# Fewer semaphore counts by TensorE, and steps of VectorE, TensorE and ScalarE put in another order, in a two-layer graph network

## The chip, the cores and the metric

One core of a Trainium2 chip runs the whole program. The metric is the device time of one execution in microseconds (us). Three runs of the kernel before gave 1814.47, 1814.22 and 1812.03 us; their median is 1814.22 us.

## The reference

A graph of 3125 nodes with 64 features and 100000 edges, sorted by their destination, goes through two layers. Cut to what matters:

```python
# layer 0 (16 edge features, edge type 0..2, node type 0..1)
h1, h2, h3, h4 = (projection of x by the node's type, for W1..W4)
w5e   = edge_feat @ W5[edge_type] + b5[edge_type]
num   = sum(h3[dst] * (h4[src] + w5e), axis=-1)
score = softmax((num / 4)[:, None], axis=-1)[:, 0]
out   = h1 + segment_sum(score[:, None] * (h2[src] + w5e), dst)
x     = layernorm(x + out)
# layer 1 (32 edge features)
m     = relu(x[src] + edge_feats @ We + be) + 1e-7
a     = exp(m - segment_max(m, dst)[dst]) / its segment_sum
x     = layernorm(x + (x + segment_sum(m * a, dst)) @ Wm + bm)
```

All arithmetic on the features is float32; rows that are fetched by a product with a one-hot matrix are split in three bf16 parts.

## The kernel before

The edges are cut in two halves, and a chunk is 512 edges of each half: channels of the first half lie on partitions 0 to 63, those of the second on 64 to 127. There are `CHUNKS` = 98 chunks (49 for each of two sets of buffers, s = c % 2, r = c // 2). Sums over the edges of a node are running scans along the edges, whose last value is fetched per node at the end.

Each engine has its own program, written out by hand, and waits on semaphores: an instruction adds to one as it ends, and another engine waits for a count. Names of semaphores say what has ended, such as `q4_ready`, `num_ready`, `runT`.

**Stage 0** (layer 0) is a loop over c on each engine, one chunk a step, with work of several chunks in each step.

- GpSimd fetches the source rows of chunk c with indirect DMAs (`gather0`, L599), 8 of them, or 6 where a quarter of the rows comes by a one-hot product (56 chunks, `PICKED`). A ring of 8 buffers lies between it and TensorE.
- TensorE in step c: `pick0` (L872, one-hot products, about 19 matmuls of 512 columns a step), `project0` of chunk c+1 (L881 and, by `add_rows`, L854 and L859), `turn_inj` of c+1 (L894), `numerator` of c (L909, turns the product for VectorE), `difference` of c (L854, L859 again), `turn_prob` of c-1 (L918), `turn_run` of c-2 (L927).
- VectorE in step c: `score_parts` of c-1 (L1184, L1187, L1190), `mask` of c+1 (L1196), `expand` of c (L1205, a scan), `products` of c (L1213), `probabilities` of c-1 (L1218, L1220, L1223), `message_sums` of c-2 (L1229, L1235, a scan), and then `one_hot0` (L1178, six or seven tiles) that a later `pick0` reads.
- ScalarE in step c: `exponents` of c-1 (L677), `copy_keep` of c (L690), which waits for the scan of c-2, `widen` of c-1 (L683), `copy_q2` of c (L696), `copy_picked` (L707), and `store0` of c-2 (L713), which copies what `turn_run` made and issues its DMA.

**Stage 1** (layer 1) is such a loop again, from c = -2 to 98.

- TensorE: `pick` (L970), `project1` of c+2 (L949, L952, L958), `turn1` of c-1 (L981), which turns two scans of 512 columns, first the sum of weights, then the sum of weighted messages.
- VectorE: `of_part` (L1294, every second step: takes the right half of a pair of one-hot rows), `maxima` of c (L1328, L1333, L1337), `summands` of c-1 (L1343), `one_hot` (L1285), `sums` of c-1 (two scans, L1353, L1358).
- ScalarE: `decays`, `store_max` and `decay` of c (L766 to L782), `store1` of c-1 (L789, two copies and a DMA), `messages` of c+2 (L759, L761, the relu that `maxima` of c+2 reads two steps later).

The lines that set the order are these two of stage 0 (TensorE, VectorE), and the last three calls of ScalarE's step in stage 1:

```python
for work, d in ((project0, 1), (turn_inj, 1), (numerator, 0), (difference, 0), (turn_prob, -1), (turn_run, -2)):
for work, d in ((score_parts, -1), (mask, 1), (expand, 0), (products, 0), (probabilities, -1), (message_sums, -2)):
```

## Time and profile before

| | |
|---|---|
| median of three runs | 1814.22 us (1812.03 to 1814.47) |
| profiled execution, span from its first to its last instruction | 2243.3 us |
| mean granted TensorE clock in it | 0.901 |
| TensorE matmuls, busy | 1756.8 us (78%), 8720 instructions |
| VectorE, busy | 1622.9 us (72%), 3313 instructions |
| GpSimd, busy | 1321.5 us (59%), 1377 instructions |
| ScalarE, busy | 785.0 us (35%), 1508 instructions |

The own time of the profiled execution is its span, 2243.3 us; what lies around the span is not told, and can only add to it. It is 429 us above the median of the runs that are not profiled. So a wait in the profile need not be in the runs at the same length, and how much of each can be in them is a question of its own. Busy times of matmuls are modelled and overlap; the starts of two matmuls tell what one costs. "remote" marks a wait that ended with a semaphore count for which no instruction that had just ended is found; "issue" marks an idle time that no wait in the profile explains.

### The profile page before, as it was taken

To read this page: it belongs to the slowest core of one execution; us is meant where nothing else is said; L and a number is where in the kernel's file an instruction comes from. 1 tells how busy PE (TensorE), PEld (TensorE's weight loads), DVE (VectorE), ACT (ScalarE), POOL (GpSimd) and SP (SyncE) were. 2 spreads that over 40 slices of the span, in tenths; PEclk is the share of its full clock that TensorE was granted. 3 is DMA by queue.
4 is the path that set the end of the run, shared out by engine and by line. 5 is a ranking of instruction groups with operands and counts; after the bars stand their busy time and mean duration, and the time that the engine had idled before them with its cause. 6 is when DMAs were issued, how large, how long until landed. Compare 5 with 4: busy or idle time off the path is not lost.

```text
span 2243.3 us, 28657 instructions
## 1 busy us (share of the span) xinstructions
PE 1756.8 (78%) x8720; PEld 1065.5 (47%) x8720; DVE 1622.9 (72%) x3313; ACT 785.0 (35%) x1508; POOL 1321.5 (59%) x1377
## 2 busy tenths in 40 slices
PE   4447988888788887889875278888888889888864
PEld 4423555555555554555544135444444545445434
DVE  6042777778777777777768558788878878879785
ACT  3110222222222222223222135555545545455551
POOL 5661566666666666666650666666666666666624
PEclk9988998999999999999987579899998999999875
DMA  7951454445454544545443235555545555555441
GB/s 252 342 129 48 124 144 131 146 138 151 135 142 146 141 148 138 148 140 147 139 128 111 53 86 154 149 152 157 157 144 158 161 141 169 150 162 155 142 145 44
DMA packets 216628, 322.18 MB, mean 144 GB/s; under 512 B 62017, under 2 KB 124026, under 8 KB 216347
## 3 DMA queue, kind: packets, MB, share of 16 engines
q1 hardware_dynamic: 128556, 147.55, 22.1%
q0 software_dynamic: 44016, 70.01, 13.6%
q10 hardware_dynamic: 43904, 102.79, 13.0%
q8 instruction: 71, 1.16, 0.2%
q14 instruction: 81, 0.66, 0.1%
HBM read 186.93 MB, written 133.22 MB: 143 GB/s over the span
## 4 chain that ended last, share of the span: by engine, by line
PE 32%; DVE 25%; issue 17%; another core or an unknown queue 15%; ACT 8%; ACTq 1%; POOL 1%; DMA 1%; DVEq 0%; SPq 0%; POOLq 0%
PE wide L970 13%; PE wide L872 5%; DVE h3d L1205 4%; PE wide L981 4%; DVE run L1235 4%; DVE late L1178 4%; DVE edge_lists L1178 3%; DVE score L1184 2%; PE bank L949 2%; DVE prod L1213 2%; ACT block L789 2%; DVE bank L1229 2%; PE bank L958 2%; PE bank L833 1%
## 5 line engine op out<-in xcount | busy, mean ns | idle before, releaser
L609 POOL DMA_INDIRECT rows<-d_x,idx x588 | 558.8, 950 | 323.0 <-issue 154.1
L599 POOL DMA_INDIRECT block<-d_h,idx x496 | 476.4, 960 | 265.0 <-issue 131.4
L970 PE MATMUL wide<-late,ntype_i 125*128 125x512 bf16 x975 | 235.2, 399 | 51.1 <-DVE ntype_i L1318 49.7
L872 PE MATMUL wide<-late,typed 125*128 125x512 bf16 x728 | 234.2, 403 | 39.0 <-issue 19.7
L599 POOL DMA_INDIRECT rows<-d_h,idx x176 | 169.0, 960 | 155.2 <-PE wide L859 51.7
L970 PE MATMUL wide<-edge_lists,ntype_i 125*128 125x512 bf16 x936 | 233.4, 406 | 9.6 <-issue 9.4
L872 PE MATMUL wide<-edge_lists,typed 125*128 125x512 bf16 x672 | 210.8, 395 | 2.8 <-issue 2.7
L981 PE MATMUL wide<-ident,block 128*128 128x128 f32 x784 | 147.3, 317 | 73.1 <-issue 56.5
L789 ACT ACTIVATE block<-wide 128x512 f32<-128x512 f32 x196 | 108.3, 592 | 266.8 <-remote 214.1
L1184 DVE TENSOR_REDUCE score<-bank 128x8 f32<-128x512 f32 x98 | 67.4, 688 | 177.9 <-remote 165.7
L690 ACT ACTIVATE keep_late<-keep 128x512 bf16<-128x512 bf16 x98 | 61.7, 630 | 353.1 <-DVE run L1235 240.8
L970 PEld LDWEIGHTS wide<-late,ntype_i 125*128 125x128 bf16 x975 | 100.1, 103 | 168.6 <-DVE ntype_i L1318 50.1
L696 ACT ACTIVATE q_sb<-wide 128x512 f32<-128x512 f32 x98 | 58.4, 596 | 299.8 <-remote 270.6
L981 PEld LDWEIGHTS wide<-ident,block 128*128 128x128 f32 x784 | 115.9, 210 | 99.6 <-issue 80.4
L970 PEld LDWEIGHTS wide<-edge_lists,ntype_i 125*128 125x128 bf16 x936 | 97.5, 104 | 130.0 <-issue 42.0
L918 PE MATMUL bank<-ident,prob_wide 128*128 128x128 f32 x392 | 67.5, 298 | 113.8 <-issue 84.6
L872 PE MATMUL wide<-late,ntype_i 125*128 125x512 bf16 x364 | 145.4, 400 | 5.4 <-issue 5.2
L872 PEld LDWEIGHTS wide<-late,typed 125*128 125x128 bf16 x728 | 74.4, 103 | 128.4 <-issue 63.0
L872 PE MATMUL wide<-edge_lists,ntype_i 125*128 125x512 bf16 x336 | 132.1, 393 | 2.0 <-issue 2.0
L1205 DVE TENSOR_TENSOR_SCAN h3d<-keep,h3d,bank 128x512 f32<-128x512 bf16 x98 | 124.8, 1274 | 8.7 <-PE bank L894 8.7
L1178 DVE TENSOR_SCALAR late<-msg,pick_of 125x512 bf16<-125x512 f16 x364 | 113.8, 376 | 21.0 <-PE wide L872 10.8
L1333 DVE TENSOR_TENSOR_SCAN h3d<-bank,h3d,keep 128x511 f32<-128x511 f32 x98 | 125.5, 1281 | 3.5
(227 smaller groups left out, 3503.6 us busy)
## 6 DMA issues: line engine op xcount, KB each, us to landing
d_run<-block ACTq DMA_DIRECT2D x98, 512.0 KB
d_inj<-zeros SPq DMA_DIRECT2D x28, 896.0 KB
inj<-d_inj SPq DMA_DIRECT2D x98, 256.0 KB
d_run<-stage ACTq DMA_DIRECT2D x98, 256.0 KB
feat<-in_ea16x3T SPq DMA_DIRECT2D x196, 96.0 KB
types<-d_type SPq DMA_DIRECT2D x196, 64.0 KB
keep<-d_keep SPq DMA_DIRECT2D x196, 64.0 KB
keep<-d_pen SPq DMA_DIRECT2D x196, 64.0 KB
```

The source lines that it names most:

```text
L599: pool.indirect_dma_start(out=ring[c % RING][:, j, h, :], out_offset=None, in_=d_h24, in_offset=bass.IndirectOffsetOnAxis(ap=idx[:, c, at: ...
L609: pool.indirect_dma_start(out=rows1[c % RING1][:, j, h, :], out_offset=None, in_=d_x1, in_offset=bass.IndirectOffsetOnAxis(ap=idx[:, c, at ...
L789: act.activation(stage1[s][:, :, :, q, :], p_out1[:, q * CH:(q + 1) * CH].rearrange("p (j h c) -> p j h c", j=TILES, h=2), ACT.Copy).then_ ...
L872: ins = pe.matmul(p_pick[s][:, 0:cols], table0[n][:, k, :], hot0[b][:, k - b * KT, 0:cols], start=(k == 0 and n == 0), stop=(k == NT - 1 a ...
L918: ins = pe.matmul(p_prob[:, j:CH:TILES], prob_wide[s][:, j, :, :].rearrange("p h c -> p (h c)"), ident[:, :], is_transpose=True, start=Tru ...
L970: ins = pe.matmul(p_hot[s], table[q][:, SPLIT * k:SPLIT * (k + 1), :].rearrange("p b c -> p (b c)"), hot[s][:, k, :], start=(k == 0 and q ...
L981: ins = pe.matmul(p_out1[:, q * CH + j * P:q * CH + (j + 1) * P], src[:, j:CH:TILES], ident[:, :], is_transpose=True, start=True, stop=True)
L1178: ins = dve.tensor_scalar(hot0[b][:, k - b * KT, 0:cols], pick_slots[u % SLOTS][0:NP, 0:cols], pick_of[:, k:k + 1], None, ALU.is_equal)
L1184: dve.tensor_reduce(score[s][:, :, :, :].rearrange("p j h a -> p (j h a)"), p_num[:, :].rearrange("p (e c) -> p e c", c=C), AX.X, ALU.add) ...
L1205: dve.tensor_tensor_scan(h3d[s][:, :], keep[s][:, :], p_inj[:, :], h3d[1 - s][:, CH - 1:CH], ALU.mult, ALU.add).then_inc(h3_ready[s], 1)
L1235: dve.tensor_tensor_scan(run[s][:, :], keep_late[s][:, :], p_prob[:, :], run[1 - s][:, CH - 1:CH], ALU.mult, ALU.add).then_inc(run_ready[s ...
L1333: dve.tensor_tensor_scan(before[s][:, 1:CH], p_m[c % 3][:, 0:CH - 1], keep[s][:, 1:CH], before[s][:, 0:1], ALU.max, ALU.add).then_inc(befo ...
```

## The change

In stage 0 TensorE no longer counts `q4_ready` (but for the last chunk, `last_rows`), `num_ready`, and `runT` (but for the last chunk, `last_turned`). Who waited for them waits for a count that TensorE makes a little later anyway: `mask` for `injT`, `score_parts` and `products` for `q2_ready`, `store0` for `probT` of the next chunk. In stage 1 `turn1` counts once for both halves (`turned`) in place of twice, and ScalarE's `store1` waits for both before its first copy. The orders change too: VectorE's stage 0 step begins with `expand` and `products`, and `message_sums` stands ahead of `probabilities`; TensorE's has `turn_run` ahead of `turn_prob`; in stage 1 VectorE does `maxima` ahead of `of_part` (the half selection), and ScalarE does `messages` (the relu) ahead of `store1`. The diff, cut to its core:

```diff
             def store0(s, r, c):
-                act.wait_ge(runT[s], r + 1)
+                if c == CHUNKS - 1:
+                    act.wait_ge(last_turned, 1)
+                else:
+                    act.wait_ge(probT[1 - s], r + s + 1)
...
             def store1(s, r, c):
                 act.wait_ge(stored[s], 16 * (EACH + r))
+                act.wait_ge(turned[s], r + 1)
                 for q in range(2):
-                    act.wait_ge(runT[s], EACH + 2 * r + q + 1)
...
+                if c + 2 < CHUNKS:
+                    messages(*chunk_of(c + 2))
                 if c >= 1:
                     store1(*chunk_of(c - 1))
-                if c + 2 < CHUNKS:
-                    messages(*chunk_of(c + 2))
...
-                add_rows(s, c, 1).then_inc(q4_ready[s], 1)
+                ins = add_rows(s, c, 1)
+                if c == CHUNKS - 1:
+                    ins.then_inc(last_rows, 1)
...
             def difference(s, r, c):
 
-                pe.wait_ge(prod_ready[s], r + 1)
                 add_rows(s, c, 0).then_inc(q2_ready[s], 1)
...
-                ins.then_inc(num_ready[s], 1)
...
-                ins.then_inc(runT[s], 1)
+                if c == CHUNKS - 1:
+                    ins.then_inc(last_turned, 1)
...
-                for work, d in ((project0, 1), (turn_inj, 1), (numerator, 0), (difference, 0), (turn_prob, -1), (turn_run, -2)):
+                for work, d in ((project0, 1), (turn_inj, 1), (numerator, 0), (difference, 0), (turn_run, -2), (turn_prob, -1)):
...
-                    ins.then_inc(runT[s], 1)
+                ins.then_inc(turned[s], 1)
...
             def score_parts(s, r, c):
 
-                dve.wait_ge(num_ready[s], r + 1)
+                dve.wait_ge(q2_ready[s], r + 1)
...
-                wait(dve, q4_ready[s], r)
+                wait(dve, injT[s], r)
...
                 dve.wait_ge(h3_ready[s], r + 1)
-                dve.wait_ge(q4_ready[s], r + 1)
-                wait(dve, num_ready[s], r)
+                if c == CHUNKS - 1:
+                    dve.wait_ge(last_rows, 1)
+                wait(dve, q2_ready[s], r)
...
-                wait(dve, runT[s], r)
...
-                for work, d in ((score_parts, -1), (mask, 1), (expand, 0), (products, 0), (probabilities, -1), (message_sums, -2)):
+                for work, d in ((expand, 0), (products, 0), (mask, 1), (score_parts, -1), (message_sums, -2), (probabilities, -1)):
...
             for c in range(-2, CHUNKS + 1):
+                if 0 <= c < CHUNKS:
+                    maxima(*chunk_of(c))
                 if c % 2 == 0 and (c + 2) // 2 < PAIRS:
                     of_part((c + 2) // 2)
-                if 0 <= c < CHUNKS:
-                    maxima(*chunk_of(c))
```

On VectorE a step in the middle of stage 0 reads so before, from one group of one-hot tiles (`edge_lists`) back to `score`:

```order
L1184 TENSOR_REDUCE score<-bank 128x8
L1187 TENSOR_REDUCE top<-score 128x8
L1190 TENSOR_TENSOR diff<-score,top 128x8
L1196 SCALAR_TENSOR_TENSOR featm<-types,type_of_row,feat 128x512
L1205 SCALAR_TENSOR_TENSOR h3d<-keep,h3d,bank 128x512
L1213 SCALAR_TENSOR_TENSOR prod<-h3d,wide 128x512
L1218 TENSOR_REDUCE total<-expo 128x8
L1220 RECIPROCAL inv<-total 128x8
L1223 TENSOR_TENSOR prob<-expo,inv 128x8
L1229 TENSOR_TENSOR bank<-bank,q_sb 128x512
L1235 SCALAR_TENSOR_TENSOR run<-keep_late,run,bank 128x512
L1178 TENSOR_SCALAR edge_lists<-msg,pick_of 125x512 x7
```

and so in the changed kernel (its line numbers are a little higher):

```order
L1210 SCALAR_TENSOR_TENSOR h3d<-keep,h3d,bank 128x512
L1219 SCALAR_TENSOR_TENSOR prod<-h3d,wide 128x512
L1201 SCALAR_TENSOR_TENSOR featm<-types,type_of_row,feat 128x512
L1189 TENSOR_REDUCE score<-bank 128x8
L1192 TENSOR_REDUCE top<-score 128x8
L1195 TENSOR_TENSOR diff<-score,top 128x8
L1235 TENSOR_TENSOR bank<-bank,q_sb 128x512
L1240 SCALAR_TENSOR_TENSOR run<-keep_late,run,bank 128x512
L1224 TENSOR_REDUCE total<-expo 128x8
L1226 RECIPROCAL inv<-total 128x8
L1229 TENSOR_TENSOR prob<-expo,inv 128x8
L1183 TENSOR_SCALAR edge_lists<-msg,pick_of 125x512 x7
```

The score, which reads what TensorE's `numerator` turned, moved from the first place to the fourth, and the three small instructions of the probabilities moved behind the scan of the messages, next to the one-hot tiles.

On ScalarE in the middle of stage 1 (`block` is the staged output and one of the relu buffers, `bank` the messages in PSUM), before:

```order
L782 DMA d_own<-block 64x512
L776 ACTIVATE bank<-prob_wide 128x512
L789 ACTIVATE block<-wide 128x8x64 x2
L792 DMA d_run<-block 128x1024
L759 ACTIVATE block<-bank 64x512
L761 ACTIVATE bank<-bank 128x512
L766 ACTIVATE prob_wide<-q_sb 128x512
```

and in the changed kernel:

```order
L786 DMA d_own<-block 64x512
L780 ACTIVATE bank<-prob_wide 128x512
L763 ACTIVATE block<-bank 64x512
L765 ACTIVATE bank<-bank 128x512
L793 ACTIVATE block<-wide 128x8x64 x2
L796 DMA d_run<-block 128x1024
L770 ACTIVATE prob_wide<-q_sb 128x512
```

The two relu instructions stand ahead of the two copies and their DMA now. The same instructions are issued on every engine as before.

## Rows read from the trace of the kernel before

**Rows 1.** The page: the span, and busy time, share and instructions of two engines.
```profile
span 2243.3 us, 28657 instructions
PE 1756.8 (78%) x8720; PEld 1065.5 (47%) x8720; DVE 1622.9 (72%) x3313; ACT 785.0 (35%) x1508; POOL 1321.5 (59%) x1377
```
**Rows 2.** Stretches of the two loops: us, each engine's busy us (instructions), clock, DMA.
```profile
226.00:1213.00 987.00, 838.91 (x4477) 526.37 (x4476) 750.73 (x1671) 272.63 (x581) 592.43 (x616) 0.94 0.49 141
1305.00:2175.00 870.00, 738.87 (x3479) 418.91 (x3478) 706.29 (x1231) 452.31 (x779) 533.72 (x564) 0.91 0.52 151
```
**Rows 3.** Who waited for whom: engine, line, releaser: us in total, times, longest.
```profile
DVE h3d L1328 <- ACT bank L761: 101.0, 19, 9.3
ACT block L789 <- remote: 214.1, 55, 8.1
POOL block L599 <- issue: 131.4, 431, 0.3
```
**Rows 4.** The chain that ended last, in stage 0: start, us, what.
```profile
709.16 3.92 another core or an unknown queue
...
721.30 0.86 another core or an unknown queue
722.19 0.69 DVE score L1184
...
730.38 3.86 another core or an unknown queue
```
**Rows 5.** Timeline in stage 0: start, us, engine, line, operation, count, [idle before].
```profile
706.44 1.02 PE L881 MATMUL wide<-featm,w 128*128 128x512 f32 x2
...
708.20 0.64 PE L909 MATMUL bank<-ident,prod 128*128 128x128 f32 x4
...
709.26 0.60 PE L918 MATMUL bank<-ident,prob_wide 128*128 128x128 f32 x4
709.70 0.64 PE L927 MATMUL bank<-ident,run 128*128 128x128 f32 x4
710.18 0.60 PE L872 MATMUL wide<-late,typed 125*128 125x512 bf16 x2
...
710.62 0.38 PE L872 MATMUL wide<-late,ntype_i 125*128 125x512 bf16 x1
...
713.10 0.69 DVE L1184 TENSOR_REDUCE score<-bank 128x8 f32<-128x512 f32 x1 [3.94 <-remote]
```
**Rows 6.** Timeline: the end of the next step, on VectorE, ScalarE and TensorE.
```profile
719.12 2.18 DVE L1178 TENSOR_SCALAR edge_lists<-msg,pick_of 125x512 bf16<-125x512 f16 x7
719.30 0.63 ACT L690 ACTIVATE keep_late<-keep 128x512 bf16<-128x512 bf16 x1 [2.87 <-DVE run L1235]
...
719.84 0.61 ACT L683 ACTIVATE prob_wide<-prob 128x512 f32<-128x512 f32 x1
...
720.50 0.95 PE L918 MATMUL bank<-ident,prob_wide 128*128 128x128 f32 x4 [2.45 <-issue]
```
**Rows 7.** Groups of VectorE's instructions in the stretch 226 to 1213 us.
```profile
L1205 DVE TENSOR_TENSOR_SCAN h3d<-keep,h3d,bank 128x512 f32<-128x512 bf16 x98 | 124.8, 1274 | 8.7 <-PE bank L894 8.7
...
L1196 DVE SCALAR_TENSOR_TENSOR featm<-types,type_of_row,feat 128x512 f32<-128x512 bf16 x96 | 71.7, 747 | 0.5 <-issue 0.3
L1184 DVE TENSOR_REDUCE score<-bank 128x8 f32<-128x512 f32 x97 | 66.7, 688 | 177.9 <-remote 165.7 <-PE bank L909 12.2
L1213 DVE SCALAR_TENSOR_TENSOR prod<-h3d,wide 128x512 f32<-128x512 f32 x97 | 66.6, 687 | 3.3
...
L1220 DVE RECIPROCAL inv<-total 128x8 f32<-128x8 f32 x96 | 19.5, 203 | 3.3
...
L1223 DVE TENSOR_TENSOR prob<-expo,inv 128x8 f32<-128x8 f32 x96 | 16.0, 167 | 3.3
...
L1218 DVE TENSOR_REDUCE total<-expo 128x8 f32<-128x8 f32 x96 | 14.8, 154 | 33.4 <-issue 19.0 <-ACT expo L677 14.2
```
**Rows 8.** Timeline of VectorE in stage 1: the first instruction of two steps.
```profile
1510.52 0.21 DVE L1328 SCALAR_TENSOR_TENSOR h3d<-bank,h3d,keep 128x1 f32<-128x1 f32 x1
...
1517.73 0.19 DVE L1328 SCALAR_TENSOR_TENSOR h3d<-bank,h3d,keep 128x1 f32<-128x1 f32 x1
```

More of the change, by code:

```diff
@@ L289, in gnn_program @@
         feat_in, keep_in, inj_in = sems("feat_in"), sems("keep_in"), sems("inj_in")
-        masked, q4_ready, q2_ready, injT = sems("masked"), sems("q4_ready"), sems("q2_ready"), sems("injT")
+        masked, q2_ready, injT, last_rows = sems("masked"), sems("q2_ready"), sems("injT"), sem("last_rows")
         keep_copied, q2_copied, h3_ready, prod_ready = sems("keep_copied"), sems("q2_copied"), sems("h3_ready"), sems("prod_ready")
-        num_ready, score_ready, diff_ready = sems("num_ready"), sems("score_ready"), sems("diff_ready")
+        score_ready, diff_ready = sems("score_ready"), sems("diff_ready")
         exps_ready, prob_ready = sems("exps_ready"), sems("prob_ready")
@@ L295, in gnn_program @@
         wide_ready, probT, msg_ready = sems("wide_ready"), sems("probT"), sems("msg_ready")
-        run_ready, runT, staged, stored = sems("run_ready"), sems("runT"), sems("staged"), sems("stored")
+        run_ready, staged, stored = sems("run_ready"), sems("staged"), sems("stored")
+        last_turned, turned = sem("last_turned"), sems("turned")
         s_cut, s_square, s_squared, s_var, s_sqrt, s_x1, s_x1_out = (sem("s_cut"), sem("s_square"), sem("s_squared"),
@@ L908, in numerator @@
                 for j in range(TILES):
-                    ins = pe.matmul(p_num[:, j * P:(j + 1) * P], prod[s][:, j:CH:TILES], ident[:, :], is_transpose=True,
-                                    start=True, stop=True)
-                ins.then_inc(num_ready[s], 1)
+                    pe.matmul(p_num[:, j * P:(j + 1) * P], prod[s][:, j:CH:TILES], ident[:, :], is_transpose=True,
+                              start=True, stop=True)
             def turn_prob(s, r, c):
@@ L936, in _ @@
                     pick0(AHEAD_PIECES + c + 1)
-                for work, d in ((project0, 1), (turn_inj, 1), (numerator, 0), (difference, 0), (turn_prob, -1), (turn_run, -2)):
+                for work, d in ((project0, 1), (turn_inj, 1), (numerator, 0), (difference, 0), (turn_run, -2), (turn_prob, -1)):
                     if chunk_of(c + d):
                         work(*chunk_of(c + d))
-            for work, back in ((numerator, 2), (difference, 2), (turn_prob, 3), (turn_run, 4), (turn_inj, 1), (project0, 1),
-                               (turn_prob, 2), (numerator, 1), (difference, 1), (turn_run, 3), (turn_run, 2), (turn_prob, 1), (turn_run, 1)):
+            for work, back in ((numerator, 2), (difference, 2), (turn_run, 4), (turn_prob, 3), (turn_inj, 1), (project0, 1),
+                               (turn_run, 3), (turn_prob, 2), (numerator, 1), (difference, 1), (turn_run, 2), (turn_prob, 1), (turn_run, 1)):
                 work(*chunk_of(CHUNKS - back))
@@ L1349, in sums @@
                 dve.wait_ge(decay_ready[s], r + 1)
-                dve.wait_ge(runT[s], EACH + 2 * r)
+                wait(dve, turned[s], r)
                 if not first:
```

## The prediction

> **What bounds the kernel now.** I first compare the profiled execution with the runs. Its span is 2243.3 us [rows 1], 429 more than the median of 1814.22, so I ask of every wait whether the runs can hold it. A measurement of this kernel tells about 0.2% (3.6 us) from no change.
>
> The stretches come next [rows 2]. The loop of stage 0 takes 987 us for 98 steps, 10.07 a step, and VectorE is busy for 750.7 of it; that of stage 1 takes 870, 8.88 a step, with VectorE busy for 706.3. So VectorE idles 236 us in the one and 164 in the other, 400 in all. Outside the loops lie 386 us, with 166 of VectorE's work.
>
> What a step costs without a wait: on VectorE the chain goes from the score at 722.19 to the end of seven one-hot tiles at 730.38, 8.19 us; the mean is 6.2 tiles (611 tiles, of about 0.31 us each by 2.18 for seven in rows 6), so 7.95. On TensorE all but the one-hot products goes from 706.44 to 710.18, 3.74 us with no gap [rows 5]; about 19 one-hot products a step at 0.22 a start (710.18 to 710.62 for two) add 4.18: 7.92. GpSimd has 616 gathers in the stretch, 592.4 us busy, with 131.4 / 431 = 0.305 us of issue for each [rows 2, 3]: 780 us, 7.96 a step. Three engines need 7.9 to 8.0 us each. In stage 1 VectorE goes from 1510.52 to 1517.73 with no wait, 7.21 us [rows 8].
>
> With no wait in either loop the span would be 2243.3 - (987 - 98 × 7.95) - (870 - 98 × 7.21) = 2243.3 - 208 - 163 = 1872 us. **The runs are below even that, by 58 us.** So most of the waits that the profile shows are not in the runs, and the balance of three engines leaves little to win.
>
> What the waits are: VectorE's score waits 177.9 us, 165.7 of it for a "remote" count [rows 7]. The chain has it alternate, 3.9 us, 0.9 us, 3.9 us [rows 4]. The place shows that it is a late count: the numerator's four matmuls start at 708.20 and take 0.64 in all, yet the score starts at 713.10 [rows 5], 4.3 us after their end, while TensorE already runs the next one-hot products. Here the count travels slowly in the profiled execution. ScalarE waits 214.1 us in the same way in front of `store1`, and `messages` stands behind it, for which VectorE waits 101.0 us [rows 3].
>
> **The change part by part.**
>
> *Counts taken away.* TensorE drops 97 counts of `q4_ready`, 98 of `num_ready`, 97 of `runT` and 98 of stage 1's second, 390 in all. A block of four transposes has a count on its last. The block at 709.26 lasts 0.60, three starts and one matmul of 0.27, so its starts lie 0.11 apart; the next block starts 0.44 after it, again 0.11 for each of four. For the block at 709.70 it is 0.64, 0.12 apart, and 0.48 to the next work [rows 5]. The start behind a counted matmul is no later than the others, within 0.01 us. I cost a count at 0; the bounds are 0 and 390 × 0.01 = 4 us. The Trainium skill (TensorE: Matmul & The Clock Gate, The cost: per-tile semaphore tail) has increments of concurrent tiles go one after another at about 26.3 ns each; an estimate by it is 390 × 26.3 ns = 10.3 us less. The rows do not show that spacing.
>
> *Score to the fourth place.* The numerator's count is now wanted behind `expand`, `products` and `mask`: 1.27 + 0.69 + 0.75 = 2.7 us later [rows 7]; waiting for `q2_ready` in its place makes it about 0.48 later (TensorE's block of `difference`, as long as that at 709.70), so 2.2 us of cover are won for this count. But a step waits for its latest count, and what is late next is known: `expand`, now first, wants `injT` of its chunk. TensorE makes that count in the same step as the old one, one block (0.44 us) sooner, and VectorE asks for it 0.52 us later after its scan, since the probabilities stand in between (next part). So a late count costs 0.96 us less than before: of waits of 3.9 us 2.9 are left, those of 0.9 vanish [rows 4]. With as many of the one as of the other that is about 0.9 us a step, 88 us of the 178 [rows 7]. Bounds: 0.44 a step, 43 us, if the later asking is no gain; all 178, if the counts are less late once fewer are made.
>
> *Probabilities behind the message sums.* `widen` on ScalarE stands behind `copy_keep`, which waits for the scan: copy at 719.30, widen at 719.84 [rows 6]. The probabilities now end 0.154 + 0.203 + 0.167 = 0.52 us after the scan [rows 7], about when ScalarE is free of the copy (0.54). Cost 0, at most 0.1 a step, 10 us. The one-hot tiles end 0.52 later against the scan.
>
> *`turn_run` ahead of `turn_prob`.* It fills TensorE's wait for `widen` (2.45 us at 720.50 [rows 6]) with 0.48 us of work. TensorE is then at the next `pick0` 0.48 sooner, and finds the one-hot tiles 0.52 later. The two cancel: 0 in the likeliest case. `store0` waits for `probT` in place of `runT`, which now ends the same group: 0.
>
> *Stage 1.* `messages` ahead of `store1` frees VectorE's 101.0 us [rows 3] from a count that only `store1` needs. `store1` starts its first copy one half later, about 0.5 us, with nobody but a DMA behind it: 0. `maxima` ahead of `of_part` lets 2 us of work pass over a late `picked` count; the product that needs `of_part` stands behind four us of one-hot products on TensorE: 0. `decays` behind `store1` are as they were.
>
> **The sum.** In the profiled execution's own time the change is worth 88 us of stage 0's wait (43 to 178) and 101 of stage 1's, less what comes back (I allow a third of the 101), so I expect its span near 2060 to 2090 us. The runs hold a part of that only. Above: the stretches outside the loops hold at least VectorE's 166 us, so the loops take 1648 us or less in a run, against 1487 with no wait: 161 us of waits at most. Below: 0, since the runs are 58 us under the span with no wait. I take 25 us, near the low end, because the row that is nearest, the 58, already asks for shorter work outside the loops than the profile has. Of 400 us of idle time the change relieves 88 + 101 = 189, 47%: 12 us. **1814 - 12 = 1802 us.**
>
> **The rivals.**
>
> *The runs have no such waits at all.* Then every engine does the same work, and 1814 comes out again, within 3 us. For it: the 58 us. Against it: two balanced engines that wait for each other in both directions seldom lose nothing. Chance 0.22.
>
> *The late counts are in the runs too.* If idle time shrank alike everywhere, the runs would keep (1814 - 1623) / (2243 - 1623) = 31% of it: 123 us in the loops, 47% of it relieved, 58 us: 1756. Against it: outside the loops the idle time is mostly of DMAs and gathers, which have no reason to shrink to a third. Chance 0.07.
>
> *The counts cost TensorE time themselves.* If it paced the loops and each count took what the nearest rows could hide (0.01 us) the gain were 4 us, 1810; by the estimate from the Trainium skill's page above, 1804. Rows 5 speak against it. Chance 0.03.
>
> *Slower: `pick0` waits for its one-hot tiles.* They end 0.52 us later after the scan. If TensorE paces a step and doesn't use the 0.48 us that it gains, because it never waited for `widen` in the runs, each step can lose 0.04 to 0.52 us: 4 to 51 over 98 steps. It decides as soon as TensorE finishes a step ahead of the tiles with no wait at `turn_prob`. I take 0.12, of short steps mixed with long: 12 us, 1826. For it: the three engines are within 0.1 us a step, and whatever ties TensorE closer to VectorE's end costs. Chance 0.16.
>
> The forecast has the other 0.52, and its own range is 1780 to 1810.
>
> **How the numbers follow.** Faster: 0.50 of the forecast's 0.52, with 0.07 and 0.03: 0.60. Same: 0.02 of it and 0.20 of the 0.22: 0.22. Slower: 0.16 and 0.02: 0.18. The range leaves out the large gain and the worst third of the slower case: from 1776 (a gain of 38, the forecast with 80 us of waits in the runs) to 1826.
>
> **What would show it.** In the changed profile the score should wait under 30 us, and the first place, `expand`, for `injT` some 90 (43 to 135 would fit). The wait of stage 1's `maxima` for the relu should be under 30. `pick0` should wait for one-hot tiles under 20 us; if it waits for more, and the runs are slower, the last rival holds. If the profile's span falls by some 170 us and the runs don't move, the waits were of the profiled execution alone. Starts of transposes that come closer than 0.109 us would prove that counts cost time.

## The result, and the profile after

The changed kernel takes 1815.58 us, median of 20 runs (1813.86 to 1826.56). The kernel before, timed beside it, takes 1813.64 (20 runs, 1812.03 to 1816.28). The ratio is 1.0013, 95% interval 1.0007 to 1.0019: the interval leaves out 1, so it is about 2 us slower, far less than would count as a change here. The profiled execution took 1815.25 us, 0.3 us from that median.

The page of the changed kernel, the same two lines as [rows 1]:

```profile
span 1813.4 us, 28558 instructions
PE 1608.3 (89%) x8720; PEld 1013.9 (56%) x8720; DVE 1626.6 (90%) x3313; ACT 792.4 (44%) x1508; POOL 1317.7 (73%) x1377
```

The span is 430 us below the one on record for before, and the runs have not moved. My prediction named that case: the waits were of that profiled execution alone. The busy times are those of before to within 1%, except TensorE's. The stretches (columns as in [rows 2], cut where the two loops lie now):

```profile
149.00:943.00 794.00, 774.48 (x4472) 510.78 (x4470) 747.26 (x1672) 279.83 (x581) 599.61 (x625) 0.99 0.63 177
1024.00:1753.00 729.00, 668.97 (x3495) 385.88 (x3492) 713.18 (x1233) 453.18 (x781) 539.55 (x572) 0.99 0.59 181
```

Stage 0 takes 8.10 us a step where [rows 2] had 10.07, stage 1 7.44 where it had 8.88. VectorE idles 47 and 16 us in the two, not 236 and 164. The two groups of VectorE that the change turns round, in 250 to 900 us (busy us, mean ns | idle before, released by):

```profile
L1210 DVE TENSOR_TENSOR_SCAN h3d<-keep,h3d,bank 128x512 f32<-128x512 bf16 x80 | 102.0, 1275 | 8.8 <-issue 7.4 <-PE bank L900 0.4
...
L1189 DVE TENSOR_REDUCE score<-bank 128x8 f32<-128x512 f32 x79 | 53.8, 681 | 0.0
```

The score of [rows 7] waits for nothing, and the scan that stands first now waits 8.8 us in 80 steps.

**A condition of the chip that has to be known.** The experiments below ran in five sessions, each on another chip and each with fresh runs of the kernel before beside them. In two of the five TensorE's counts reached the other engines some us late, as in [rows 4, 5], and there the kernel before took about 2240 us, with or without the profiler. In the other three, and in the timing above, it took 1814, and no profile shows late counts. So the record's profile of before is of the late condition and its timed runs are not. I compare times only within a session, and say which condition it had.

The count may not be all that is late. Ahead of the loop of that profile TensorE starts one-hot products 2.10 us apart and waits for nothing that the profile shows, where `e1_again` (below) starts them 0.22 apart (start, us, ..., [idle before]):

```profile
173.77 0.58 PE L872 MATMUL wide<-late,typed 125*128 125x512 bf16 x1 [2.38 <-issue]
...
175.87 0.58 PE L872 MATMUL wide<-late,ntype_i 125*128 125x512 bf16 x1 [1.52 <-issue]
```

What causes the condition stays open. I go on calling it "late counts".

### The profile page after: what moved, and what is told of

Read it like the earlier page. It is cut to its first block, busy times and chain, and to the rows that moved or that the text cites. A ratio compares the mean times of both kernels' runs of the same rounds, so it can differ in the third digit from the quotient of the medians.

```text
span 1813.4 us, 28558 instructions
## 1 busy us (share of the span) xinstructions
PE 1608.3 (89%) x8720; PEld 1013.9 (56%) x8720; DVE 1626.6 (90%) x3313; ACT 792.4 (44%) x1508; POOL 1317.7 (73%) x1377
## 4 chain that ended last, share of the span: by engine, by line
PE 40%; POOL 38%; issue 13%; DMA 3%; SPq 3%; DVE 2%; ACT 1%; ACTq 0%; DVEq 0%; POOLq 0%
POOL rows L610 31%; PE wide L876 20%; POOL block L600 4%; PE wide L885 4%; PE wide L858 4%; PE bank L914 2%; PE bank L931 2%; PE bank L900 2%; PE bank L922 2%; DMA d_inj<-zeros 1%; POOL typed L630 1%; POOL d_inj L620 1%; SPq L451 1%; PE bank L830 1%; PE wide L863 1%
## 5 line engine op out<-in xcount | busy, mean ns | idle before, releaser
L975 PE MATMUL wide<-late,ntype_i 125*128 125x512 bf16 x975 | 220.2, 381 | 49.7 <-DVE ntype_i L1323 49.7
L876 PE MATMUL wide<-late,typed 125*128 125x512 bf16 x728 | 219.7, 384 | 18.8 <-DVE late L1183 18.8
L975 PE MATMUL wide<-edge_lists,ntype_i 125*128 125x512 bf16 x936 | 209.9, 379 | 0.0
L876 PE MATMUL wide<-edge_lists,typed 125*128 125x512 bf16 x672 | 200.0, 379 | 0.0
L975 PEld LDWEIGHTS wide<-edge_lists,ntype_i 125*128 125x128 bf16 x936 | 91.9, 98 | 100.2
L780 ACT ACTIVATE bank<-prob_wide 128x512 f32<-128x512 f32 x98 | 59.0, 602 | 196.1 <-DVE block L1363 192.8
L876 PE MATMUL wide<-late,ntype_i 125*128 125x512 bf16 x364 | 139.4, 383 | 0.0
L1240 DVE TENSOR_TENSOR_SCAN run<-keep_late,run,bank 128x512 f32<-128x512 bf16 x98 | 125.4, 1280 | 3.5
L876 PE MATMUL wide<-edge_lists,ntype_i 125*128 125x512 bf16 x336 | 127.3, 379 | 0.0
L1358 DVE TENSOR_TENSOR_SCAN block<-bank,block 128x512 f32<-128x512 f32 x98 | 124.3, 1268 | 1.8 <-ACT bank L780 1.8
L986 PE MATMUL wide<-ident,block 128*128 128x128 f32 x784 | 114.7, 290 | 10.4 <-DVE block L1358 5.3
L1363 DVE TENSOR_TENSOR_SCAN block<-bank,block,run 128x512 f32<-128x512 f32 x98 | 122.7, 1252 | 0.0
```

The source lines that it names most:

```text
L876: ins = pe.matmul(p_pick[s][:, 0:cols], table0[n][:, k, :], hot0[b][:, k - b * KT, 0:cols], start=(k == 0 and n == 0), stop=(k == NT - 1 a ...
L975: ins = pe.matmul(p_hot[s], table[q][:, SPLIT * k:SPLIT * (k + 1), :].rearrange("p b c -> p (b c)"), hot[s][:, k, :], start=(k == 0 and q ...
L986: ins = pe.matmul(p_out1[:, q * CH + j * P:q * CH + (j + 1) * P], src[:, j:CH:TILES], ident[:, :], is_transpose=True, start=True, stop=True)
L1240: dve.tensor_tensor_scan(run[s][:, :], keep_late[s][:, :], p_prob[:, :], run[1 - s][:, CH - 1:CH], ALU.mult, ALU.add).then_inc(run_ready[s ...
L1358: dve.tensor_tensor_scan(run_s[s][:, :], p_decay[:, :], expm[s][:, :], run_s[1 - s][:, CH - 1:CH], ALU.mult, ALU.add).then_inc(s_run[s], 1)
L1363: dve.tensor_tensor_scan(run_n[s][:, :], p_decay[:, :], mexp[s][:, :], run_n[1 - s][:, CH - 1:CH], ALU.mult, ALU.add).then_inc(n_run[s], 1)
```

## The experiments

### Is the profile of before the kernel that was timed?

`e1_again` is the kernel before with no edit.

> The kernel before, unchanged, profiled once more. Theory A (the late counts of TensorE are a state of one profiled execution, and the runs have none): the span comes out near 1812 us, stage 0's loop near 794 us, and the score's waits for a remote count under 20 us in all. Theory B (the late counts come with this kernel's number of counts whenever it is profiled, and fewer counts end them): the span comes out near 2240 us again. Either way the time of the run without a profile should be 1812 to 1816 us.

It took 1814.02 us, beside 1813.72 for before (27 runs). Its page and two stretches, one inside each loop (columns as in [rows 2]):

```profile
span 1812.2 us, 28657 instructions
PE 1627.7 (90%) x8720; PEld 1028.7 (57%) x8720; DVE 1628.7 (90%) x3313; ACT 784.9 (43%) x1508; POOL 1318.7 (73%) x1377
...
250.00:750.00 500.00, 500.00 (x2906) 327.16 (x2904) 482.70 (x1088) 178.39 (x371) 379.47 (x396) 1.00 0.61 177
1100.00:1650.00 550.00, 526.40 (x2680) 304.83 (x2679) 544.85 (x956) 334.61 (x588) 415.62 (x442) 1.00 0.65 185
```

The same stretches of the changed kernel:

```profile
250.00:750.00 500.00, 500.00 (x2910) 327.57 (x2909) 480.58 (x1089) 178.50 (x372) 379.57 (x396) 1.00 0.63 177
1100.00:1650.00 550.00, 511.10 (x2678) 292.86 (x2676) 544.88 (x957) 340.70 (x588) 415.89 (x441) 1.00 0.60 184
```

The kernels are alike here to within a few instructions (TensorE's busy time in stage 1 differs by 15 us; ends of matmuls are modelled). In stage 0 TensorE has no idle time in 500 us. VectorE is busy for 483. GpSimd shows 379, but each of its gathers has issue time in front of it that isn't counted as busy (the waits of `e1_again`, and the gathers of stage 1 with shortest/median/longest ns and first and last start):

```profile
POOL block L599 <- issue: 150.6, 494, 0.3
POOL rows L609 <- issue: 178.9, 587, 0.3
...
L609 POOL DMA_INDIRECT rows<-d_x,idx x588: 940/944/2314, 1002.0 to 1737.4; - x196
```

150.6 / 494 is 0.305 us. With 396 gathers that is 121 us more, and 379 + 121 = 500: GpSimd is full too. In stage 1 the 588 gathers start over 735.4 us, 1.253 us apart on the mean. Nearly all are 0.944 + 0.305 = 1.249 us apart, six a step 7.49 us; the rest is a few longer ones at the start. The changed kernel's 588 gathers start over the same length, 1001.3 to 1736.6.

VectorE is full beside it: 544.85 of the 550 us, far from the 7.21 us a step of [rows 8]. Its 73 steps in that stretch (L1328) start from 1107.0 to 1646.4 us, 7.49 apart like GpSimd's. So a step of stage 1 has no idle time in it that an order could take away, on either engine. What decides the end is GpSimd: VectorE starts the last chunk at 1744.1, 6.7 us after the last gather starts.

Stage 0 ends in the same way. Its gathers start ahead of the loop:

```profile
L599 POOL DMA_INDIRECT rows<-d_h,idx x176: 940/944/1455, 52.3 to 938.4; - x176
```

The first scan of the loop starts at 149.4 us, 97 us after the first gather; the last scan starts at 943.5, 5.1 after the last. In between GpSimd waits for a buffer 0.6 us in all (25 gathers of another kind, L619, stand among these). Its lead is used up when the stage ends. The time of the whole program is then 52.3 us before the gathers, 886.1 of gathers for stage 0, 63.6 between, 735.4 of gathers for stage 1 and 74.8 behind them: 1812.2. **The gathers of GpSimd, which the change doesn't touch, set the end of both stages.** The runs that leave work out, below, bear on this.

### The parts of the change alone (no late counts)

`e2_counts` takes 293 of the 390 counts from the kernel before (it keeps `runT` of stage 0) and leaves all orders:

```diff
-                add_rows(s, c, 1).then_inc(q4_ready[s], 1)
+                ins = add_rows(s, c, 1)
...
-                ins.then_inc(num_ready[s], 1)
...
-                    ins.then_inc(runT[s], 1)
+                ins.then_inc(turned[s], 1)
...
-                dve.wait_ge(num_ready[s], r + 1)
+                dve.wait_ge(q2_ready[s], r + 1)
```

> The kernel before with 293 of the 390 counts of TensorE taken away (q4_ready, num_ready and the second of each turn1 in stage 1), every order as before. Theory A (a count costs nothing and nobody waits for one in the runs): within 3 us of before. Theory C (counts cost TensorE time, 0.026 us each): 7.7 us faster. If the profiled execution spans about 1812 us while that of the kernel before spans 2240 again, the number of counts decides the state of the profiled execution.

Measured 1819.9 us, ratio 1.003 (1.002 to 1.0039): 6 us slower, outside the 3 us of theory A and not the way of theory C. The score still stands first, and waits for a later count. The group of the score in 250 to 900 us, first of `e2_counts`, then of `e1_again`:

```profile
L1186 DVE TENSOR_REDUCE score<-bank 128x8 f32<-128x512 f32 x79 | 54.0, 684 | 7.7 <-PE wide L860 4.9 <-PE wide L855 0.9
```

```profile
L1184 DVE TENSOR_REDUCE score<-bank 128x8 f32<-128x512 f32 x79 | 53.8, 682 | 3.8 <-PE bank L909 3.0
```

From the first scan of stage 0 to the last it takes 797.9 us, `e1_again` 794.1. That is 3.8 us, as much as the two profiled spans differ (1815.5 and 1812.2); where the rest of the 6 lies they don't show. In the whole change the score is fourth and this cost is gone: 792.8. Fewer counts gave nothing back.

`e3_orders` is the other half: all the new orders, with every count kept.

```diff
-                for work, d in ((score_parts, -1), (mask, 1), (expand, 0), (products, 0), (probabilities, -1), (message_sums, -2)):
+                for work, d in ((expand, 0), (products, 0), (mask, 1), (score_parts, -1), (message_sums, -2), (probabilities, -1)):
```

> The kernel before with all orders of the change (stage 0 of VectorE and TensorE, stage 1 of VectorE and ScalarE), and all counts kept. Theory A (in the runs each engine is kept busy by its own work, so an order moves nothing): within 3 us of before. Theory D (the one-hot tiles, which end 0.5 us later against the scan, hold up TensorE): 2 to 12 us slower, with a wait of the one-hot products for VectorE in the profile. My recorded forecast of the orders' gain, 12 us, should not come out under either.

Measured 1815.42 us, ratio 1.0007 (0.9998 to 1.0016): no difference that can be told. It also prices the counts without the score's later wait: with all 390 of them this kernel takes 1815.42, without them the changed kernel takes 1815.58 (another session, same before), so 390 counts fewer are worth nothing that can be told.

`e4_orders1` is before with the two orders of stage 1 alone:

```diff
-                if c >= 1:
-                    store1(*chunk_of(c - 1))
                 if c + 2 < CHUNKS:
                     messages(*chunk_of(c + 2))
+                if c >= 1:
+                    store1(*chunk_of(c - 1))
...
-                if c % 2 == 0 and (c + 2) // 2 < PAIRS:
-                    of_part((c + 2) // 2)
                 if 0 <= c < CHUNKS:
                     maxima(*chunk_of(c))
+                if c % 2 == 0 and (c + 2) // 2 < PAIRS:
+                    of_part((c + 2) // 2)
```

> The kernel before with the two orders of stage 1 alone (maxima ahead of the half selection on VectorE, relu ahead of the stores on ScalarE). Theory A: within 2 us of before, since stage 1 is paced by GpSimd's six gathers a step, 6 x 1.25 = 7.5 us. Theory E (relu comes late in the runs too): some us faster. With e3 it tells the two stages apart: if e3 is slower and this is not, stage 0's order costs.

Measured 1816.57 us, ratio 1.0011 (1.0002 to 1.002): 2.9 us slower, a little outside the 2 us of theory A, and not faster as theory E has it.

### The same parts with late counts

In the first late session before takes 2240.24 us (17 runs). `f1_more_counts` is before with 1176 counts added on a semaphore that nobody waits for, on the first three of each four transposes in stage 0:

```diff
+                    if j < TILES - 1:
+                        ins.then_inc(extra, 1)
```

> The kernel before with 1176 counts more on TensorE: every transpose of stage 0's four blocks of four adds to a semaphore that nobody waits for. Theory A (a count costs nothing): within 3 us of before. Theory C (0.026 us each): 31 us slower, and starts of transposes 0.135 us apart. If counts make those behind them late, the profiled span goes up as in the trace of before, towards 2240 us.

Measured 2252.27, ratio 1.0053 (1.0038 to 1.0067): 12.0 us for 1176 counts, 0.010 us each. Its timeline of four blocks of transposes (start, us, ...), beside the three of [rows 5]:

```profile
706.83 0.60 PE L895 MATMUL bank<-ident,inj 128*128 128x128 f32 x4
707.26 0.64 PE L912 MATMUL bank<-ident,prod 128*128 128x128 f32 x4
...
708.33 0.60 PE L923 MATMUL bank<-ident,prob_wide 128*128 128x128 f32 x4
708.76 0.64 PE L934 MATMUL bank<-ident,run 128*128 128x128 f32 x4
```

Blocks with a count on each matmul start 0.43 us apart, where [rows 5] has 0.44 with one count in four. So TensorE's starts don't pay, and the 12 us sit in waits. The score's:

```profile
DVE score L1193 <- remote: 196.9, 80, 6.4
```

That is 31 us more than the 165.7 of [rows 7]. By the rule cited in the prediction (the Trainium skill, TensorE: Matmul & The Clock Gate, The cost: per-tile semaphore tail), 1176 increments of 26.3 ns would be, as an estimate, 30.9 us if each lay on the path. The trace shows no such spacing of starts. The late wait grew by as much, but two executions in this condition also differ by themselves, so I don't take that as agreement.

`f4_orders0` is before with stage 0's orders of VectorE and TensorE, all counts kept: the line of VectorE shown for `e3_orders`, and

```diff
-                for work, d in ((project0, 1), (turn_inj, 1), (numerator, 0), (difference, 0), (turn_prob, -1), (turn_run, -2)):
+                for work, d in ((project0, 1), (turn_inj, 1), (numerator, 0), (difference, 0), (turn_run, -2), (turn_prob, -1)):
```

> The kernel before with stage 0's orders of VectorE and TensorE alone, all counts kept. From the two profiles with all orders, which are 2 us shorter in stage 0 and 2 us longer in stage 1 than before: 1 to 3 us faster than before, if those differences are real; within 1 us of before if they are not.

Measured 2240.73, ratio 1.0003 (0.9991 to 1.0015). The score's wait has gone over to the scan that stands first (waits: us in total, times, longest):

```profile
DVE h3d L1205 <- issue: 172.4, 68, 5.6
```

In a second late session (before 2244.34, 17 runs) `g1_after` is the changed kernel with no edit.

> The changed kernel once more. The last call showed that the same kernel before takes 2240 us in every run of one session on the chip and 1813 in another, with counts of TensorE that come up to 5 us late in the first. In a session without late counts: 2 us slower than before, as measured. In a session with late counts, theory A (the waits only move from the score to expand, as in the profile with stage 0's orders, 178 us then 172 us): within 0.5% of before. Theory H (fewer counts make the others less late; 1176 more cost 12 us, so 390 fewer may give 4 us): 4 us or more faster.

Measured 2253.22, ratio 1.0045 (1.0029 to 1.006): the change is slower where its waits exist. Page, and three groups of the whole run:

```profile
span 2247.0 us, 28558 instructions
...
L1210 DVE TENSOR_TENSOR_SCAN h3d<-keep,h3d,bank 128x512 f32<-128x512 bf16 x98 | 125.1, 1276 | 190.6 <-issue 178.6 <-PE bank L900 8.4 <-remote 3.3
L1348 DVE SCALAR_TENSOR_TENSOR run<-bank,block 128x512 f32<-128x512 f32 x98 | 67.0, 684 | 94.3 <-ACT block L774 51.8 <-issue 42.2
...
L1189 DVE TENSOR_REDUCE score<-bank 128x8 f32<-128x512 f32 x98 | 66.9, 683 | 19.9 <-remote 19.9
L1333 DVE SCALAR_TENSOR_TENSOR h3d<-bank,h3d,keep 128x1 f32<-128x1 f32 x97 | 18.6, 192 | 16.3 <-ACT bank L765 14.8 <-issue 1.4
```

The score waits 20 us in place of 178, the relu's reader 16 in place of 101 ([rows 3, 7]), both as the prediction said. But the scan, now first, waits 191 (8.7 in [rows 7]). In stage 1 the sum of the messages, which reads ScalarE's exponentials, waits 94. Those stand behind `store1` still, and `store1` still stands behind the late count. **Both waits moved by one place and about kept their size.** (VectorE's `run` L1343 waits 0.8 us in the record's profile of before, so the 94 us are new.)

The two stages did not come out alike. From the first scan of stage 0 to the last it takes 975.8 us in `g1_after` and 976.1 in `f4_orders0`, against 985.5 in the record's profile of before; from the first to the last chunk of stage 1 (L1333) 870.0, against 858.1 there and 856.2 in `f4_orders0`, which has stage 1 as before. So in the late condition the orders of stage 0 seem to win about 10 us, of the 88 that I had put, and those of stage 1 to lose about 12. These are single executions, and the median of `f4_orders0` shows no gain; stage 1's orders were never undone in a late session.

### What is a wait worth, and an engine's work?

These leave work out. `pick2` drops the third of three one-hot products (the third bf16 part of the table isn't added); `pick2_mask` computes the mask on 16 of 512 columns besides (the rest of the masked features is 0); `g5` fetches five blocks of 128 rows a step in stage 1 in place of six, so that one block of the gathered rows is stale. All are edits of the changed kernel.

```diff
-                    for n in range(3):
+                    for n in range(2):
...
```

```diff
-                dve.scalar_tensor_tensor(featm[s][:, :], types[s][:, :], type_of_row[:, :], feat[s][:, :],
+                dve.scalar_tensor_tensor(featm[s][:, 0:16], types[s][:, 0:16], type_of_row[:, :], feat[s][:, 0:16],
...
```

```diff
-                    for j in range(PE_J):
+                    for j in range(PE_J - h):
...
-                pe.wait_ge(got_rows[c % RING1], rows_of_stage0(c % RING1) + 16 * 2 * PE_J * (c // RING1 + 1))
+                pe.wait_ge(got_rows[c % RING1], rows_of_stage0(c % RING1) + 16 * (2 * PE_J - 1) * (c // RING1 + 1))
```

In the two sessions with late counts:

> The changed kernel with two of the three one-hot products of each tile in stage 0 (the smallest bf16 part of the fetched rows is left out): TensorE has about 6.9 x 0.216 = 1.5 us less to do in a step. Theory A (TensorE, VectorE and GpSimd are all near their limit in stage 0): only 5 to 25 us faster, VectorE's step then sets the pace at 8.0 to 8.2 us. Theory F (TensorE alone paces stage 0): up to 91 x 1.5 = 135 us faster.

> The changed kernel with five of the six gathers of each step of stage 1 (one block of 128 rows of the second half is not fetched and stays as it was in the buffer): GpSimd has 1.25 us less to do in a step. Theory A (GpSimd paces stage 1, with VectorE close behind at 7.2 us of work against 7.5): 20 to 30 us faster, paced by VectorE. Theory G (VectorE or the waits between engines pace it): less than 5 us faster.

`f2_pick2`: 2231.21, ratio 0.9964 (0.9949 to 0.9978). `f3_after_g5`: 2126.59, 0.95 (0.9483 to 0.9517).

> The changed kernel with five of the six gathers of each step of stage 1 (a block of 128 rows of the second half isn't fetched). With late counts it was 114 us faster than before. In a session without late counts, theory A (GpSimd paces stage 1, VectorE is close behind): 20 to 30 us faster than before. Theory G (GpSimd doesn't pace it): under 5 us.

> The changed kernel with two of the three one-hot products of each tile in stage 0 (the smallest bf16 part is left out). With late counts 9 us faster than before. In a session without late counts, theory A (TensorE, VectorE and GpSimd are all near their limit): 5 to 25 us faster; theory F (TensorE alone paces stage 0): up to 135 us faster.

> As the run before, and VectorE's mask works on 16 of 512 columns (the other columns of the masked features are zero), some 0.6 us less for VectorE in a step. In a session without late counts, theory A: faster than the run before by 10 to 40 us, until GpSimd's 7.9 us a step end it. If VectorE's work isn't a limit: no faster than the run before.

`g2_g5`: 2125.0, 0.9462 (0.9441 to 0.9482). `g3_pick2`: 2229.63, 0.9937 (0.9916 to 0.9957). `g4_pick2_mask`: 2227.56, 0.992 (0.99 to 0.994). Against the changed kernel of the same session (`g1_after`, 2253.22) one gather fewer a step is worth 128 us, and a third of the one-hot products 24. As an estimate, 98 gathers at 1.249 us each are 122: VectorE idles in this condition and can follow. The late condition holds up GpSimd too, which waits for counts before it may refill a buffer (waits of `g1_after` in stage 1):

```profile
POOL rows L610 <- remote: 112.6, 50, 3.9
```

These sizes say nothing of the timed condition. The same three without late counts (before 1813.83, 14 runs):

> The changed kernel with five of the six gathers of each step of stage 1, a block of 128 rows of the second half left out; the same kernel was 0.947 of before in two sessions with late counts. In a session without them, theory A (GpSimd paces stage 1, VectorE close behind at 7.2 us of work): 20 to 30 us faster than before; theory G (waits between the engines pace it): under 5 us. If the counts are late again: 2117 to 2127 us, as before.

> The changed kernel with two of the three one-hot products of each tile in stage 0, the smallest bf16 part left out. In a session without late counts, theory A (three engines near their limit): 5 to 25 us faster than before; theory F (TensorE alone paces stage 0): up to 135 us faster. If the counts are late again: 2227 to 2234 us.

> As the run before, with VectorE's mask on 16 of 512 columns, the others zero, some 0.6 us less for VectorE in a step. In a session without late counts, theory A: another 10 to 40 us faster, until GpSimd's 7.9 us a step end it; if VectorE's work is no limit, no faster than the run before. If the counts are late again: 2224 to 2228 us.

`h2_pick2`: 1811.28, ratio 0.9986 (0.9977 to 0.9996). `h3_pick2_mask`: 1806.38, 0.9963 (0.9949 to 0.9977). `h1_g5`: 1799.03, 0.9923 (0.9906 to 0.9939). Against the 1815.58 of the changed kernel that is 4, 9 and 17 us (it was timed in another session, whose runs of before agree with these: 1813.64 and 1813.83). Against before `h2_pick2` gains 2.6 us, `h3_pick2_mask` 4.9 more and `h1_g5` 14.8, all below what theory A had (5 to 25, 10 to 40 more, 20 to 30). The stretch of stage 0 in `h2_pick2`, and that of stage 1 in `h1_g5`:

```profile
250.00:750.00 500.00, 442.17 (x2536) 290.69 (x2534) 486.63 (x1109) 174.94 (x378) 378.44 (x400) 1.00 0.64 179
```

```profile
1100.00:1650.00 550.00, 529.88 (x2730) 308.83 (x2728) 544.75 (x975) 345.92 (x597) 356.40 (x374) 1.00 0.59 184
...
POOL rows L610 <- PE bank L963: 111.8, 82, 1.8
```

With TensorE relieved by 58 us in 500, GpSimd is still full (378.4 + 400 × 0.305 = 500.4) and 4 us is all that comes. Where they come from the gathers of stage 0 show, in the changed kernel, `h2_pick2` and `h3_pick2_mask`:

```profile
L600 POOL DMA_INDIRECT rows<-d_h,idx x176: 940/944/1441, 52.7 to 937.9; - x176
...
L600 POOL DMA_INDIRECT rows<-d_h,idx x176: 940/945/1438, 52.3 to 933.9; - x176
...
L600 POOL DMA_INDIRECT rows<-d_h,idx x176: 940/944/1042, 52.2 to 928.0; - x176
```

The same 672 gathers take 885.2, 881.6 and 875.8 us, and the last scan of the stage starts 4.1, 4.1 and 3.0 us behind the last of them. The gains of 4 and 9 us are nearly all gathers that became a little shorter while other engines did less (why they did was not tried), and hardly anything else of the work left out shows in the time. In `h3_pick2_mask` TensorE (L858) waits for gathered rows 79.8 us in 44 times, in the changed kernel 10.0 in 4: what it gains it waits for GpSimd.

In `h1_g5` GpSimd has 1.25 us a step less to do, and the step shrinks by 0.17: VectorE's first and last chunk of stage 1 start 698.0 us apart, before the edit 713.9. That difference of 15.9 us is nearly the whole gain. GpSimd now waits for buffers, and VectorE starts the last chunk 22.8 us after the last gather starts (6.9 in the changed kernel): GpSimd no longer sets the end, VectorE does. But VectorE was full before the edit too (544.88 of 550 us) and is so after it (544.75), so its own work must have become shorter. It did: in 1100 to 1650 us a step goes from 7.49 to 7.36 us, and its 6.5 one-hot tiles a step from 0.328 us of busy time each to 0.307 (one group of each in the last section), 0.14 a step. So the gain can't be put down to GpSimd's shorter work alone, and no run relieved VectorE alone in stage 1.

So in stage 0 TensorE and GpSimd are full (500 of 500 us each, TensorE's modelled) with VectorE at 483, and in stage 1 GpSimd is full and VectorE has 5 us in 550 to spare.

### Where the last 2 us are

The changed kernel's stage 0 is no longer than `e1_again`'s (792.8 us against 794.1), its gathers take as long (735.3 and 735.4), but from the last gather's start to the end it is 76.8 us against 74.8. VectorE's waits for ScalarE's exponentials at the end, 1700 to 1760 us, in the changed kernel and in `e1_again`:

```profile
DVE run L1348 <- ACT block L774: 3.4, 4, 1.1
```

```profile
DVE run L1343 <- ACT block L770: 0.8, 1, 0.8
```

At the end VectorE has no more one-hot tiles to make and the steps come closer together, and the exponentials have the relu and the stores ahead of them. The last two runs undo that, in a session without late counts (before 1813.87, 23 runs). `k1_act_undone` has ScalarE's order back, `k2_orders1_undone` both orders of stage 1:

```diff
-                if c + 2 < CHUNKS:
-                    messages(*chunk_of(c + 2))
                 if c >= 1:
                     store1(*chunk_of(c - 1))
+                if c + 2 < CHUNKS:
+                    messages(*chunk_of(c + 2))
```

> The changed kernel with ScalarE's order of stage 1 as before (the stores ahead of the relu). Theory J (the changed kernel's 2 us are the drain behind the last gather, in which VectorE now waits up to 1.1 us a step for ScalarE's exponentials, which stand behind the relu): from the last gather to the end 75 us in place of 77, and 2 us faster than the changed kernel, so within 1 us of before. Theory K (the 2 us are of the counts or of stage 0): no faster than the changed kernel, 1.0013 of before. With late counts: it tells whether this order is what makes the changed kernel 1.0045 of before there; if so, it comes within 0.2% of before.

> As the run before, with VectorE's order of stage 1 as before too (the half selection ahead of the maxima). Theory J: as the run before, within 1 us of before. If VectorE's order has the 2 us, this one is faster than the run before by as much. With late counts: theory H (fewer counts and stage 0's orders help) under 1.000 of before, theory A within 0.2% of it.

Measured 1814.7 us, ratio 1.0007 (0.9999 to 1.0016), and 1814.19, ratio 1.0006 (0.9997 to 1.0014). In both the 3.4 us are 0.8 again, and the ends take 75.3 and 76.3 us. `e4_orders1`, which has these orders alone, took 76.5, `e2_counts`, which has none of them, 74.9. It fits that the orders of stage 1 cost about 1 us at the end, but the 76.3 of `k2_orders1_undone` doesn't, and the intervals overlap with that of the whole change, so it isn't settled. No version tried here that does all the work beats the kernel before.

## Why the prediction was wrong

**The step that failed** is "I take 25 us" of waits in the runs, of which 12 would be relieved. The profile without late counts has next to none: the score waits 3.8 us in 80 steps before, the scan 8.8 after. The rival "The runs have no such waits at all", 1814 within 3 us, is what happened (1815.58), and the time lies within my range. I had the argument in hand, the runs 58 us below the span with no wait, and still kept 25 us on the ground that balanced engines wait for each other. What the change can relieve is not on the path that sets the time: GpSimd works through its 886 and 735 us of gathers without waiting, VectorE is full in stage 1, and its 3.5% of idle time in stage 0 (483 of 500) leaves GpSimd's gathers where they are.

**An engine left out.** For a step of stage 1 without waits I took VectorE's 7.21 us and never multiplied GpSimd's gathers: by [rows 2, 3], 533.72 / 564 = 0.946 us busy and 0.305 of issue, 6 × 1.25 = 7.5 us. In stage 0 I had done it. With that the span with no wait would have been 28 us longer, the runs 86 below it in place of 58, and the case for waits in the runs weaker still. Nor did I follow GpSimd's gathers from one end of a stage to the other; in stage 0 I reckoned them by the step of the loop alone, though they start ahead of it. The rest was in stretches outside the loops, which I took as having "no reason to shrink": the first scan of stage 0 starts at 149 us without late counts, at 226 in [rows 2].

**Late count relief, 0.96 us a step.** Mostly wrong where it could be tried (about 10 us of the 88, as far as single profiles tell). The counts that the new first place wants are as late as the old ones: `g1_after`'s 191 us of waits at the scan against 178 before at the score; I had put 90. (The span that I expected, 2060 to 2090 us, came in neither condition: 1813 and 2247.) I had reckoned that a count asked for later in the step is less late. But what VectorE does in the meantime is the same work in another order, and the next step's TensorE work hangs on its end. My reading is that in a ring of engines the lateness goes round once a step wherever it is met; the runs show only that the wait moved. The same holds for stage 1: the 101 us turned up as 94 behind the exponentials; I had allowed for a third.

**Counts at 0.** Right as far as can be told. The block spacing of `f1_more_counts` shows no price, and `e3_orders` and the changed kernel, 390 counts apart, take the same time. Not foreseen was that waiting for a count 0.5 us later costs about 4 us of stage 0 as long as the score stands first (`e2_counts`, 6 us slower in all). In the whole change the order covers it.

**Probabilities and `turn_run`.** Right at 0 by the whole: stage 0 became 1.3 us shorter. The slower rival, `pick0` waiting for its tiles, didn't come: TensorE has no idle time from 250 to 750 us at all, and its wait for those tiles is the first one alone, ahead of the loop:

```profile
PE wide L876 <- DVE late L1183: 18.8, 1, 18.8
```

What little is lost seems to be at the other end of the program, in a place that I had costed at 0 ("frees VectorE's 101.0 us ... with nobody but a DMA behind it"); the exponentials are behind it.

## What to carry to other kernels

Before reading a wait in a profile, hold its span against the timed runs; if they differ by a fifth, the waits belong to something that the runs don't have, and the sum of work per engine and step, issue time included, is the better guide. Do that sum for every engine and every stage, from the first instruction that can run ahead to the last: here two or three engines were within 4% of each other, and taking a third of the one-hot products from one gave 4 us. When a relieved engine gives a gain, look whether the others' own instructions became shorter too. Moving the waiting instruction down its engine's order moved the wait here, in both stages, to whatever took its place.

## What the runs showed of the hardware

- A whole session can have TensorE's counts arrive late. The same program then takes 2240 us in place of 1814, 24% more, at a granted clock of 0.90 on the mean in place of 0.95. The clock alone isn't it: in `g1_after` it is 0.98 from 226 to 1213 us, and a step of stage 0 still takes 10 us. Every run of such a session was so, whatever the kernel, and each session ran on another chip. Whether it goes with the chip or with the hour was not found out.
- In that condition one gather fewer in six was worth 128 us; without it 17. A size measured in the one condition doesn't carry over to the other.
- VectorE's one-hot tiles in stage 1 take 394 ns with six gathers a step and 373 with five (the same group in 1100 to 1650 us, changed kernel and `h1_g5`). In both kernels a tile takes from 332 to about 570 ns. The gathers are issued by GpSimd; what the two share was not tried.

```profile
L1290 DVE TENSOR_SCALAR late<-zeros,slot_of 125x512 bf16<-125x512 f16 x247 | 81.0, 394 | 0.0
```

```profile
L1290 DVE TENSOR_SCALAR late<-zeros,slot_of 125x512 bf16<-125x512 f16 x247 | 75.6, 373 | 0.0
```

- An indirect gather of 128 rows occupies GpSimd for 0.944 us and 0.305 of issue, and 588 of them start over 735.2 to 735.5 us, 1.253 us apart on the mean, in every profile without late counts that has them all.
